# Context values of two latent attentions projected in the stage ahead of each; contexts normalised in the first stage; an earlier GpSimd drain

## What is computed

```python
def _L0_xattn_ref(x, latents, ln1_w, ln1_b, ln2_w, ln2_b, Wq, Wkv, Wo):   # x: the context
    xn = _layernorm(x, ln1_w, ln1_b)
    latn = _layernorm(latents, ln2_w, ln2_b)
    q = latn @ Wq                                   # 16 heads of 64
    kv = jnp.concatenate([xn, latn], axis=1) @ Wkv
    k, v = jnp.split(kv, 2, axis=-1)
    ...
    weight = jax.nn.softmax((q * scale) @ (k * scale).T)
    return (weight @ v) @ Wo
```

## Time and profile before

| | |
|---|---|
| median of 3 runs | 3015.24 us (3014.14 to 3017.68) |
| the profiled execution itself | 3041.37 us |
| its span, first to last instruction | 3039.6 us |
| mean granted TensorE clock | 0.981 |
| busy: PE, DVE, ACT, POOL | 93%, 63%, 40%, 12% |
| stage 0 (layer 0) begins | 18.0 us |
| layer 1 begins | 355.8 us |
| layer 4 begins | 1248.7 us |

### The profile page before, as it was taken

The page is one execution under the profiler, slowest core; times in us unless marked ns, Lnnn a source line. Parts: engine busy times, 40 slices in busy tenths (PEclk is TensorE's granted clock), DMA queues, the critical chain, the costliest instruction groups (busy, mean ns, idle before and its releaser), DMA issues. The chain is left out here.

```text
span 3039.6 us, 51543 instructions
## 1 busy us (share of the span) xinstructions
PE 2818.1 (93%) x20436; PEld 1809.8 (60%) x20436; DVE 1913.5 (63%) x3469; ACT 1224.9 (40%) x2599; POOL 361.8 (12%) x483
## 2 busy tenths in 40 slices
PE   6999899999998879899999999999898899989898
PEld 3566456666666758566666657766565333346576
DVE  3766367777764237477777754346557999966522
ACT  1333354445542235444545432134242766633111
POOL 1111100000002620000000000113211000001232
PEclk9999999999999989999999999999999999999899
DMA  3001010000012222100000000000000000000241
GB/s 117 17 17 69 19 37 5 5 5 5 5 67 74 79 85 88 49 5 5 5 5 9 36 18 1 27 20 24 18 21 32 18 1 1 1 18 18 101 168 66
DMA packets 43245, 103.55 MB, mean 34 GB/s; under 512 B 4929, under 2 KB 32687, under 8 KB 39425
## 3 DMA queue, kind: packets, MB, share of 16 engines
q1 hardware_dynamic: 37217, 86.66, 8.1%
q0 software_dynamic: 5792, 13.59, 1.5%
HBM read 66.74 MB, written 19.07 MB: 28 GB/s over the span
## 5 line engine op out<-in xcount | busy, mean ns | idle before, releaser
L2417 ACT ACTIVATE prob<-R,neg_max 128x333 f32<-128x333 f32 x512 | 268.4, 537 | 184.3 <-DVE neg_max L2484 184.0
L3965 DVE TENSOR_TENSOR_SCAN arena<-arena,u 128x512 f32<-128x512 f32 x256 | 289.6, 1203 | 0.1
L2305 PEld LDWEIGHTS T<-const,prob 128*128 128x128 f32 (+1 forms) x1536 | 183.1, 143 | 82.4 <-DVE prob L2497 37.1
L2497 DVE TENSOR_TENSOR prob<-prob,rec 128x666 f32<-128x666 f32 x256 | 218.4, 853 | 19.9 <-issue 0.9
L2484 DVE TENSOR_REDUCE neg_max<-R 128x2 f32<-128x666 f32 x256 | 205.9, 846 | 34.9 <-PE R L2294 34.8
L2305 PE MATMUL T<-const,prob 128*128 128x128 f32 (+1 forms) x1536 | 210.5, 273 | 13.0 <-DVE prob L2497 10.7
L2424 ACT ACTIVATE prob_t<-T 128x384 f32<-128x384 f32 x256 | 125.5, 490 | 228.1 <-PE T L2305 222.0
L3896 ACT ACTIVATE arena<-delta,neg_a 128x510 f32<-128x510 f32 x256 | 177.0, 714 | 49.0 <-DVE arena L3965 48.1
L2490 DVE COPY prob_t<-T 128x384 f32<-128x384 f32 x256 | 142.3, 556 | 38.9 <-PE T L2305 14.3
L2224 PE MATMUL O<-keys_in,arena 128*128 128x333 f32 x512 | 164.8, 444 | 0.0
L3799 PE MATMUL R<-arena,diag 64*64 64x512 f32 x1024 | 135.0, 618 | 26.5 <-DVE arena L3965 26.3
(11 more groups left out here) (595 smaller groups left out, 5444.8 us busy)
## 6 DMA issues: line engine op xcount, KB each, us to landing
w<-w_dram SPq DMA_DIRECT2D x16, 1024.0 KB
arena<-pack_dram SPq DMA_DIRECT2D x2, 4100.0 KB, 14.6
q_pad<-q_pad SPq DMA_DIRECT2D x24, 224.0 KB, 2.7
arena<-pack_dram SPq DMA_DIRECT2D x4, 1284.0 KB, 6.6
arena<-pack_dram SPq DMA_DIRECT2D x1, 4896.0 KB, 15.3
slots_in<-x_nat SPq DMA_DIRECT2D x2, 2048.0 KB, 8.2
arena<-planes SPq DMA_DIRECT2D x8, 512.0 KB, 8.5
arena<-k_nat SPq DMA_DIRECT2D x16, 224.0 KB, 2.7
```

The costliest lines, as they stand in the source:

```text
L2305: last = nc.tensor.transpose(S.T[0:n, i, kc * P:(kc + 1) * P], prob[:, g % 2, i, first:first + n], S.ident)
L2417: last = nc.scalar.activation(prob[:, g % 2, i, :], S.R[:, g % 2, i * BANK:i * BANK + XK], ACT.Exp, bias=neg_max[:, g % 2, i:i + 1], accum ...
L2497: nc.vector.tensor_tensor(prob[:, g % 2, :, :], prob[:, g % 2, :, :], rec[:, g % 2, :].unsqueeze(2).to_broadcast([P, 2, XK]), ALU.mult)\
L3965: nc.vector.tensor_tensor_scan(state[:, q % HELD, :], decay[:, q % DEEP, :], u[:, i % 2, :], 0.0, ALU.mult, ALU.add)\
```

## The change

SyncE also loads the five tiles of context rows, between x_nat and ctx_t. In layer 0 VectorE and GpSimd normalise them, TensorE transposes them ahead of the first features (its keep_warm there is halved) and ScalarE writes `ctx_hat`. In the tail of layer 0 ScalarE scales the contexts with layer 1's weights (`act_scaled`), TensorE computes w0 to w5 in place of six keep_warm calls (`value`, into the bank S_q one after the other), ScalarE copies each, and SyncE stores three tiles. Layer 3 does the same for w0 to w3 of layer 4, in four banks, in place of three keep_warm calls. `perceiver` has no c jobs; its FIRST is the rest of the w jobs, then lat, q0, v0, k0. Its lat waits until the early stores have landed (`kept`, `raw_sb`). In layer 2 turned(0) and turned(1) move behind the last second choices, and GpSimd drains once right after its last scatter.

```diff
+CTX_TILES = [(t, min(P, B * CTX - t * P)) for t in range(-(-B * CTX // P))]
+def context_rows(S):
+    return [S.xres[:, 0, :], S.xres[:, 1, :], S.yn[:, 0, :], S.yn[:, 1, :], S.ysb[:, 0, :]]
+EARLY_VALUES = {1: 6, 4: 4}
+def early_scaled(S, k):
+    at = sum(n for _, n in PACK[k].values())
+    return S.arena[k % 2][:, at:at + C * B * CTX].rearrange("p (c n) -> p c n", c=C)
+def early_tile(S, k, t):
+    at = PACK[k - 1]["nat" if "nat" in PACK[k - 1] else "wq"][0]
+    return S.arena[(k + 1) % 2][:, at + t * XI:at + (t + 1) * XI]
+def act_scaled(nc, S, act, k):
+    act.wait_ge(S.weights_ready[k], 16)
+    ctx_w, ctx_b = part(S.arena[k % 2], PACK[k], "ctx_w"), part(S.arena[k % 2], PACK[k], "ctx_b")
+    for c in range(C):
+        last = nc.scalar.activation(early_scaled(S, k)[:, c, :], S.ctx_hat[:, c, :], ACT.Identity, bias=ctx_b[:, c:c + 1], scale=ctx_w[:, c:c + 1])
+    return last
+def pe_value(nc, S, k, n, bank):
+    wkv = part(S.arena[k % 2], PACK[k], "wkv", C)
+    t, rows = CTX_TILES[n // 2]
+    for c in range(C):
+        last = nc.tensor.matmul(bank[0:rows, :], early_scaled(S, k)[:, c, t * P:t * P + rows],
+                                wkv[:, c, XI + n % 2 * BANK:XI + (n % 2 + 1) * BANK], start=(c == 0), stop=(c == C - 1))
+    return last
+def act_value(nc, S, k, n, bank):
+    t, rows = CTX_TILES[n // 2]
+    return nc.scalar.activation(early_tile(S, k, t)[0:rows, n % 2 * BANK:(n % 2 + 1) * BANK], bank[0:rows, :], ACT.Copy)
+def sync_values(nc, S, sp, k):
+    for t, n in CTX_TILES[0:EARLY_VALUES[k] // 2]:
+        sp.wait_ge(S.marks.odd_sb, 2 * (t + 1))
+        sp.dma_start(S.v_dram[t * P:t * P + n, :], early_tile(S, k, t)[0:n, :]).then_inc(S.marks.kept, 16)
+    settle(sp, S.marks.odd_sb, EARLY_VALUES[k])
...
@@ -1152,6 +1208,8 @@
             for b in range(1, B):
                 keys(b)
                 queries(b)
+            if early:
+                sync_values(nc, S, sp, k + 1)
...
@@ -1257,7 +1320,12 @@
                     product(i - 1)
                 if i + 1 < B:
                     queries(i + 1)
-                if i == 0 or i >= B:
+                if early and i == B:
+                    value(0)
+                elif early and i == B + 1:
+                    value(1)
+                    value(2)
+                elif i == 0 or i >= B:
                     keep_warm(nc, S, bank(0) if i else S.O[:, 0, :], 2)
...
                     transposed(i - 2)
-            keep_warm(nc, S, bank(0), 2)
+            if early:
+                value(3)
+            else:
+                keep_warm(nc, S, bank(0), 2)
...
             for i in range(B + 2):
+                if early and i == B - 1:
+                    act_scaled(nc, S, act, k + 1).then_inc(M.d_done, 1)
...
@@ -1330,8 +1407,16 @@
                     evacuate(i, 1)
                 if i + 2 < B:
                     keys(i + 2)
+                if early and i == B:
+                    value(0)
+                if early and i == B + 1:
+                    value(1)
+                    value(2)
                 if 0 <= i - 2 < B:
                     transposed(i - 2)
+            if early:
+                value(3)
+                settle(act, M.odd_full, EARLY_VALUES[k + 1])
...
@@ -1520,6 +1609,7 @@
                     queries(i + 1)
                 if i + 1 == B - 1:
                     prefetch(nc, S, sp, k + 1)
+            sync_values(nc, S, sp, k + 1)
             settle(sp, M.pads, 1)
             settle(sp, M.k_sb, B)
             settle(sp, M.q_sb, B)
...
+            def contexts():
+                settle(pe, M.cn_ready, 1)
+                for t, n in CTX_TILES:
+                    for c in range(C):
+                        last = nc.tensor.transpose(S.R[:, t // 4, (t % 4 * C + c) * P:(t % 4 * C + c) * P + n],
+                                                   ctx_n[t][0:n, c * P:(c + 1) * P], S.ident[0:n, 0:n])
+                last.then_inc(M.first_done, 1)
             def features(i, j):
                 name = f"f{j}"
                 if (i, name) in mixed_at:
                     mixed_free(i, name)
                     if i == -AHEAD and j == 0:
+                        contexts()
                         pe.wait_ge(S.x_ready, 32)
-                        keep_warm(nc, S, bank(0), 4)
+                        keep_warm(nc, S, bank(3), 2)
                     pe.wait_ge(M.feat_ready, i + 3)
...
@@ -1732,8 +1840,10 @@
                 if before:
                     maxima_transposed(i - 1)
                 written(i, 0)
-                if i in (B, B + 1):
-                    keep_warm(nc, S, S_q, 2)
+                if i == B:
+                    value(2)
...
+                    act_scaled(nc, S, act, k + 1).then_inc(M.d_done, 1)
+                    value(0)
...
+            nc.vector.memset(cmv[:], 1.0)
+            settle(dve, M.c_in, 16 * len(CTX_TILES))
+            for t, n in CTX_TILES:
+                nc.vector.bn_stats(cst[0:n, t, :], ctx_n[t][0:n, :])
+            dve.drain()
+            for t, n in CTX_TILES:
+                last = nc.vector.bn_aggr(cmv[0:n, t, :], cst[0:n, t, :])
+            last.then_inc(M.c_stat, 1)
+            settle(dve, M.c_rstd, 1)
+            for t, n in CTX_TILES:
+                last = nc.vector.tensor_scalar(ctx_n[t][0:n, :], ctx_n[t][0:n, :], cmv[0:n, t, 0:1], crs[0:n, t:t + 1],
+                                               ALU.subtract, ALU.mult)
+            last.then_inc(M.cn_ready, 1)
             for i in range(-AHEAD, B + 4):
...
+            settle(pool, M.c_stat, 1)
+            nc.gpsimd.tensor_scalar(crs[:], cmv[:, :, 1], EPS, None, ALU.add)
+            pool.drain()
+            nc.gpsimd.tensor_tensor(crs[:], crs[:], part(S.const, CONST, "neg_half")[:, 0:len(CTX_TILES)], ALU.pow).then_inc(M.c_rstd, 1)
...
-    CONTEXTS = (("c0", "c1", "c2", "c3", "c4") if contexts else ()) + ("w0", "w1", "w2", "w3", "w4", "w5", "w6", "w7", "w8", "w9")
+    CONTEXTS = (("c0", "c1", "c2", "c3", "c4") if contexts else ()) + tuple(f"w{n}" for n in range(early, 2 * len(LC)))
...
@@ -2159,7 +2322,7 @@
         lat = spare[:, at:at + TT * D].rearrange("p (t d) -> p t d", t=TT)
         at += TT * D
         ctx_n = spare[:, at:at + len(LC) * D].rearrange("p (t d) -> p t d", d=D)
-        ctx_s = spare[:, at:at + C * NC].rearrange("p (c n) -> p c n", c=C)
...
                     sp.dma_start(ctx_n[0:n, t, :], S.ctx_dram[t * P:t * P + n, :]).then_inc(M.c_in, 16)
-            for t, n in LC:
+            if early:
+                settle(sp, M.kept, 16 * (early // 2))
+                sp.sem_inc(M.raw_sb, 1)
+            for t, n in LC[early // 2:]:
                 sp.wait_ge(M.first_done, ctx_v_done(t))
                 sp.dma_start(S.v_dram[t * P:t * P + n, :], ctx_v[t][0:n, :]).then_inc(M.v_full, 16)
...
@@ -2425,6 +2594,8 @@
                                      S.T[:, 1, 0:3 * P].rearrange("p (c q) -> p c q", c=3), ACT.Copy).then_inc(M.pt_act, 1)
             act.wait_ge(S.weights_ready[k], 16)
+            if early:
+                context(0).then_inc(M.cnt_sb, 1)
...
@@ -2944,11 +3115,9 @@
             second_choices(1)
             residual(6)
             second_choices(2)
-            turned(0)
-            turned(1)
             residual(7)
             second_choices(3)
-            for b in range(2, B):
+            for b in range(B):
                 turned(b)
             pe.sem_inc(G.past_all, 1)
...
@@ -4610,6 +4780,9 @@
                 sp.dma_start(S.const[:], dram["const"]).then_inc(loaded, 16)
                 prefetch(nc, S, sp, layers[0])
                 sp.dma_start(S.x_nat[:], dram["x"].rearrange("(t p) d -> p t d", p=P)).then_inc(S.x_ready, 16)
+                if layers[0] == 0:
+                    for t, n in CTX_TILES:
+                        sp.dma_start(context_rows(S)[t][0:n, :], S.ctx_dram[t * P:t * P + n, :]).then_inc(S.marks.c_in, 16)
                 sp.dma_start(S.ctx_t[:], dram["ctx_t"].rearrange("(c p) n -> p c n", p=P)).then_inc(S.x_ready, 16)
...
-            lambda k: perceiver(nc, S, k, k == 1 or layers[0] > 1),
...
-            lambda k: perceiver(nc, S, k, k == 1 or layers[0] > 1),
+            lambda k: block16(nc, S, k, DH16 ** -0.5, layers[0] == 0),
+            lambda k: perceiver(nc, S, k, layers[0] > 0 and (k == 1 or layers[0] > 1), EARLY_VALUES[k] if layers[0] == 0 else 0),
...
```

More of the change, by code:

```diff
@@ L1100, in _, with block16 @@
             settle(pool, M.ln_stat, B)
-def block16(nc, S, k, scale):
+def block16(nc, S, k, scale, early):
     W, TB, M = S.arena[k % 2], PACK[k], S.marks
@@ L1880, in _ @@
                     maxima(i - 1)
+                if i == B:
+                    value(2)
+                if i == B + 1:
+                    value(5)
                 line_parts(i, 0, 0)
@@ L1891, in _ @@
                 line_parts(i, 1, 1)
+                if i == B - 1:
+                    act_scaled(nc, S, act, k + 1).then_inc(M.d_done, 1)
+                    value(0)
+                if i == B:
+                    value(3)
```

(11 more changed lines are left out.)

52 lines of the change are left out of this document (46 added, 6 removed).

## The result

The changed kernel takes 2983.61 us (median of 4 runs, 2979.28 to 2984.80), the kernel before 3015.18 in runs beside it (3014.14 to 3017.68): ratio 0.9886, 95% interval 0.9871 to 0.9902. That is 31.6 us less, where 35.2 were forecast and 2980 was named. In a second set of runs the same kernel took 2979.8 against 3016.8 (ratio 0.9887, 0.9870 to 0.9904), 37.0 less; the forecast lies between the two.

The account below looks back on a forecast made before the run. Taken to bound the kernel: the timeline at four stage edges, not TensorE's 93% mean. -21.9 - 9.2 + 2.2 - 6.3 = -35.2 us, 3006.2 from the profiled 3041.37, scaled to the runs' median: 2980, range 2974 to 2990.

Parts of the forecast that it names:

- The four edges: Edited stage edges: start, heads of both latent attentions, experts' end; work moved into idle stretches shortens the span one for one.
- First latent attention, -21.9: Layer 1's head: contexts' preparation and six of ten value jobs leave, so first scores at 369.9 instead of 391.81.
- Second latent attention, -9.2: Layer 4's head: four value jobs, a ScalarE wait and the clock's fall save 11.0; the stage ahead ends 1.8 later.
- Moved work hidden: Stages ahead: value jobs replace warm matmuls, copies and normalising fall in idle time; 5.3 us would show without ScalarE's cover.
- Rival (d): First stage's tail: waits for ScalarE let the clock fall, up to 67 us more, in full 3047; chance 0.02.
- (c): Values not hidden: stage tails stretch by 5.3 us, or the clock falls at the second edge; 2983 to 2986, chance 0.06.
- the 7.8 us of cover: First stage: VectorE free from 24.3 to 32.06, hiding 5.7 us of context normalising with 2 us to spare.
- The start, +2.2: Kernel start: five context row transfers at 0.43 us each delay everything after; bounds 0 and +8.
- The experts, -6.3: Experts' tail, layer 2: early drain removes GpSimd's 6.54 us gap, last copy ends at 1119.4; bounds -0.6 and -7.
- Rival (a): Experts' tail: early drain buys nothing, the engine being held until a moment set by transfers; gain 29.5, 2985.7, chance 0.17.
- the reorder: Experts' tail: TensorE no longer stands at quarter 0's transposes ahead of the last residual; VectorE goes straight on.

Follow-up runs that it names:

- 6: Changed kernel with layer 1's value jobs back in layer 1, contexts still normalised in the first stage: 3019.73 us beside 3041.14 for the kernel before, ratio 0.9930.
- 5: Changed kernel with layer 4's values all projected in layer 4 again and layer 3's warm matmuls back: 2994.51 us, ratio 0.9922 to the kernel before.
- 2: Changed kernel with the first two transposes back ahead of the last residual in the experts' tail, early drain kept: 2980.94 us, ratio 0.9877.
- 7: The kernel before, unaltered, profiled a second time: 3013.72 us, span 3011.9.
- 4: Changed kernel with the five context row transfers issued at the head of the first stage, not ahead of ctx_t: 2977.91 us, ratio 0.9870.
- 1: Changed kernel without the early GpSimd drain, new order of the experts' tail kept: 2987.87 us, ratio 0.9899 to the kernel before.
- 10: Changed kernel with 20 tiny matmuls (40 matmul rows) added behind the experts' last transposes: 3011.85 us beside 3041.14 for the kernel before, ratio 0.9908.
- 11: Kernel before with 44 tiny matmuls (88 matmul rows) added ahead of layer 3: 3019.27 us beside 3016.64, one run each.
- 3: Changed kernel without the early drain and with the old order of the transposes: 2986.72 us, ratio 0.9904 to the kernel before.
- 8: Changed kernel with warm matmul pairs added in the experts' tail and at layer 3's head: 2987.81 us, ratio 0.9907, beside 2979.8 for the changed kernel.

## Why the prediction was right

The four edges came out as forecast. That the whole did so too is in part luck, as the last paragraph of this section shows.

**First latent attention, -21.9**: measured -21.9, and 6 shows its two halves, 12.9 and 9.0. The price of a value job (1.74), and the piece from lat to scores read off the other attention (7.19), both held exactly.

**Second latent attention, -9.2**: -10.9 at the head against 11.0, +1.5 at the stage's end against 1.8, so -9.4. The clock's part was real: with the values left in place it fell again (5).

**Moved work hidden**: yes in both tails, for the values. Rival (d) didn't occur; of (c) the fall of the clock at the second edge did, in one profile of ten (2). At the start the account is weaker than the prediction had it. In the changed kernel's first profile VectorE's normalising ran from 26.25 to 33.43 and its next instruction came at 34.11 when ScalarE was ready: it took 7.2 us, not 5.7, and was hidden with 0.7 us to spare, not 2. TensorE's transposes of the contexts and one warm pair ended 0.4 us later than the two pairs had, and 0.6 earlier in the second profile. But the 7.8 us of cover were read off one profile with a late clock. Where the clock rises early the first lines start 13.3 us behind the stage's start (5) instead of 10.0 (7): 3.3 us that the sum doesn't hold. It came up in one of eleven profiles of changed kernels, and an early rise in two of three of the kernel before; whether the change makes it rarer is open.

**The start, +2.2**: +2.0 in the first profile and +2.2 to +2.8 in the eight others that load the rows there. The row with 14.14 us decided rightly. The page of the Trainium skill that I weighed against it ("DMA: Bandwidth & Descriptors", "Issuing engines are not separate DMA queues") calls issuing time usually small beside the DMA itself; here five issues that carry 616 rows moved the begin of the first stage by 2 us and more, and most of it was saved by moving them (4).

**The experts, -6.3**: -6.15 against the first profile, -7.1 to -7.4 against the later ones; the difference goes with the moment at which the clock fell there, in the kernel before too. Rival (a) fell in 1. One part of the reasoning was loose: I gave the reorder a share, and beside the early drain it has none (2).

**What was left out**: the measured terms make -21.9 - 9.4 + 2.2 - 6.2 to -7.1 = -35.3 to -36.2, the two sets -31.6 and -37.0. The sum had no term for layer 3's loop, whose instructions the change doesn't touch before its last iterations. It took 111.3 and 112.6 us in the two profiles of the kernel before, and 115.1 to 118.7 in ten profiles of changed kernels. 0.2 to 2.4 us of that are the gaps' place (10, 11). Part of the rest goes with the clock: the time lost to half clock in the loop (one minus the granted clock, summed over it) is 7 and 11 us before and 11 to 18 in the changed kernels, most of all (17.8) where the loop took 118.7. But not all of it: the second profile of the kernel before and the first of the changed one lose 11.2 and 11.0 us to the clock, and the loop takes 112.6 and 115.7. What makes the loop longer is open: taking back the experts' tail (3), layer 3's values (5) or the half clock at the edge (8), each by itself, didn't shorten it to what it was. The first stage takes 336.9 to 339.6 us in the changed kernels, 334.1 to 337.9 before. Elsewhere they gain some of it, likewise in code that wasn't changed: the last layer takes 197.6 to 199.7 us in all but one of them against 201.2 to 201.3 in three profiles of the kernel before. These differences, none of them in the sum, roughly cancel; so the whole came out near it partly by luck.

## To carry to other kernels

Work that depends on nothing recent belongs where warm matmuls stand in for it: there it replaces instructions of the same length, and its price at the old place is read off directly, so many jobs by their duration. Read the piece that remains from another stage in which it already stands alone. Idle time that is to hide work should be read from several profiles: here it was 7.8 us in one and 3.7 in another. And a stretch that reads "issue" behind a tiny instruction may be a cost that can be paid earlier: ask what that engine had been doing before.

## What the hardware showed beyond that

The first drain on GpSimd behind 78 indirect transfers takes its own time, 6.54 us to the digit in five profiles, even where the engine had been idle for 12.7 or 13.55 us in between; begun early it is invisible.

TensorE stops for 0.2 to 1.9 us at fixed counts of its instructions, one mark in 127 or 128 matmul rows, each with its weight load; at marks where the rows are long little or nothing shows. It shows where matmuls are tiny (64 x 64 by 17 columns, 16 ns apart, and 16 x 64 by 64 columns, 12 ns apart). The profile's page points to what it is: 166 packets, 2.72 MB, thus 16.4 KB each, against 167 before.

```profile
q8 instruction: 166, 2.72, 0.4%
```

TensorE's records in the two traces, those of its sequencer included, number 42656 and 42762, which is 166.6 and 167.0 times 256. And in layer 3 one of these packets starts 1.0 to 1.4 us behind the end of each such stop on products or scores. That the stops come from fetching instructions is inferred from this, not tested by itself.

The Trainium skill, "Runtime: NRT & Kernel Launch", section "Instruction fetch mechanics", says that instructions are fetched in blocks of 16 KiB, 256 instructions, and that crossing a boundary is mostly hidden. The size agrees with 128 rows and as many weight loads, and with the packets; if these stops are that crossing, "mostly hidden" doesn't hold in a loop of tiny matmuls, where it costs up to 1.9 us a time. Either way, 40 matmul rows fewer in one layer move the stops of another.

The clock follows idle time loosely. Behind the same 2.02 us of idle in the first stage it fell in three of the fourteen profiles and held in the others, and in two of the three profiles of the kernel before it rose some 14 us earlier at the start, with that stage 3.7 us shorter. Differences of 3 us between two profiles are nothing until a stretch with the same clock shows them.
